# Exchanging normalised rows between partitions inside SBUF in place of through a DRAM scratch, in a fused cross-attention and LoRA-expert kernel

## The reference

```python
x = x + xattn(layernorm(x), ctx, mask)      # scores, masked softmax over 64 tokens, readout
x = x + ffn(layernorm(x), W, lora_A, lora_B, router_w)

def ffn(x, W, A, B, router_w):              # 8 experts of rank 16, the top 2 of them weighted
    base = x @ W.T                          # (1024 -> 1024)
    w_dense = renormalised top-2 of softmax(x @ router_w.T)
    Ax = einsum('nd,erd->ner', x, A)
    return base + einsum('ner,ne,eor->no', Ax, w_dense, B) * 2.0
```

## Time and profile before

| | us |
|---|---|
| median of 3 runs | 1101.16 (1099.96 to 1102.52) |
| the profiled execution | 1104.84 |
| its span | 1103.1 |
| PE matmul busy in it | 1077.6 (98%) |
| DVE busy | 750.8 (68%) |
| ACT busy | 464.5 (42%) |
| POOL busy | 114.3 (10%) |

### The profile page before, as it was taken

How to read it: one execution, slowest core, us unless ns; L and a number is a source line. 1 busy time by engine, 2 the same in 40 slices (tenths; PEclk the granted TensorE clock), 3 DMA queues, 4 the chain that set the end, 5 groups by cost and what they waited for, 6 DMA issues and landing times.

```text
span 1103.1 us, 18440 instructions
## 1 busy us (share of the span) xinstructions
PE 1077.6 (98%) x6240; PEld 1041.5 (94%) x6240; DVE 750.8 (68%) x2047; ACT 464.5 (42%) x954; POOL 114.3 (10%) x282
## 2 busy tenths in 40 slices
PE   7899999999999999999999999999999999999998
PEld 6799999999999999999999999899999999999997
DVE  6866866667666677667667677567677667666662
ACT  6544344343444453444443443443443443434330
POOL 3511001010010010010010010010010010100100
PEclk9999999999999999999999999999999999999999
DMA  9364454653545553653545534554534744435322
GB/s 325 125 220 154 153 162 146 180 189 132 177 146 159 181 183 124 194 164 131 185 159 174 190 130 136 190 190 144 189 112 156 219 147 158 135 132 191 125 87 96
DMA packets 80046, 178.92 MB, mean 162 GB/s; under 512 B 9856, under 2 KB 45184, under 8 KB 80000
## 3 DMA queue, kind: packets, MB, share of 16 engines
q1 hardware_dynamic: 79568, 176.82, 47.9%
q10 hardware_dynamic: 432, 1.57, 0.4%
HBM read 111.77 MB, written 66.58 MB: 162 GB/s over the span
## 4 chain that ended last, share of the span: by engine, by line
DVE 35%; DMA 32%; ACT 13%; SPq 6%; issue 5%; POOL 5%; PE 2%; POOLq 0%; ACTq 0%; DVEq 0%
DMA xq<-xn_dram 18%; DMA xn_dram<-xn 13%; DVE x L689 7%; DVE x2T L707 7%; DVE stats L695 7%; DVE xT_lo L714 7%; SPq L316 6%; ACT xn L484 6%; POOL rstd L393 3%; ACT xT_hi L490 3%; DVE mean_var L698 1%; ACT xT_hi L460 1%; POOL shift L396 1%; DVE var_eps L700 1%; DVE ctx_lo L603 1%
## 5 line engine op out<-in xcount | busy, mean ns | idle before, releaser
L845 PE MATMUL base_ps<-w_hi,xT_hi 128*128 128x388 f32 x1512 | 530.6, 351 | 6.9 <-DVE xT_lo L714 5.0
L846 PE MATMUL base_ps<-w_lo,xT_hi 128*128 128x388 f32 x1512 | 512.0, 339 | 0.0
L847 PE MATMUL base_ps<-w_hi,xT_lo 128*128 128x388 f32 x1512 | 511.7, 338 | 0.0
L845 PEld LDWEIGHTS base_ps<-w_hi,xT_hi 128*128 128x128 f32 x1512 | 286.2, 189 | 20.8 <-DVE xT_lo L714 5.0
L846 PEld LDWEIGHTS base_ps<-w_lo,xT_hi 128*128 128x128 f32 x1512 | 285.1, 189 | 2.7
L847 PEld LDWEIGHTS base_ps<-w_hi,xT_lo 128*128 128x128 f32 x1512 | 284.2, 188 | 0.0
L484 ACT ACTIVATE xn<-x,shift,rstd 128x1024 f32<-128x1024 f32 x63 | 78.4, 1244 | 314.8 <-POOL shift L396 314.8
L490 ACT CAST xT_hi<-x2T 128x512 fp32r<-128x512 f32 x126 | 72.0, 618 | 156.0 <-DVE x2T L707 156.0
L707 DVE STREAM_TRANSPOSE x2T<-xq 128x512 f32<-128x512 f32 x126 | 82.2, 690 | 53.6 <-DMA xq<-xn_dram 53.6
L393 POOL TENSOR_TENSOR rstd<-var_eps,neg_half 128x1 f32<-128x1 f32 x64 | 36.0, 563 | 699.8 <-DVE var_eps L700 699.8
L714 DVE TENSOR_TENSOR xT_lo<-x2T,xT_hi 128x512 fp32r<-128x512 f32 x126 | 81.4, 687 | 35.2 <-ACT xT_hi L490 34.4
(11 more groups left out here) (98 smaller groups left out, 1112.9 us busy)
## 6 DMA issues: line engine op xcount, KB each, us to landing
out<-x SPq DMA_DIRECT2D x64, 512.0 KB, 3.4
x<-in_x SPq DMA_DIRECT2D x63, 512.0 KB, 5.2
xn_dram<-xn SPq DMA_DIRECT2D x63, 512.0 KB, 2.6
xq<-xn_dram SPq DMA_DIRECT2D x252, 128.0 KB, 3.0
xT_raw<-in_xT SPq DMA_DIRECT2D x62, 512.0 KB, 4.8
ctx_raw<-in_ctx SPq DMA_DIRECT2D x16, 256.0 KB, 7.8
w_raw<-in_wT SPq DMA_DIRECT2D x8, 386.0 KB, 8.4
ctxT_raw<-in_ctxT SPq DMA_DIRECT2D x8, 256.0 KB, 7.1
```

Source lines behind the costliest of these rows:

```text
L845: pe.matmul(out_, a_hi, w_h, start=start, stop=False, skip_group_check=again)
L846: pe.matmul(out_, a_hi, w_l, start=False, stop=False, skip_group_check=again)
L847: return pe.matmul(out_, a_lo, w_h, start=False, stop=stop, skip_group_check=again)
```

## The change

The scratch is gone, and with it one of the two hops. SP waits for `xn` and at once issues four transfers from `xn` to `xq`. Each reads 1 KB from each of the 128 partitions and writes 4 KB to each of 32 partitions.

The rows are spread differently. The 128 source partitions are laid out in order over 32 partitions with four places each, so partition n of a group holds rows 4n to 4n+3. A 32x32 block, which stands for one place g, has to come out at columns g, g+4, g+8 and so on of `x2T`. The transposes of DVE therefore write with a step of four fp32 elements (16 bytes), where they wrote neighbouring elements before.

In SP's order the four transfers now stand where the transfer to the scratch stood, ahead of the store of tile t, and nothing of the exchange stands behind the store.

```diff
-            def xn_out(tile):
+            def exchange(tile):
                 sp.wait_ge(xn_done, count(tile, 1, 1))
-                sp.dma_start(xn_dram, xn[:, :]).then_inc(xn_stored, 16)
-
-            def xq_in(tile):
-                sp.wait_ge(xn_stored, count(tile, 16))
                 for a in range(Q):
                     sp.dma_start(xq[a * QP:(a + 1) * QP, :, :],
-                                 xn_dram[:, a * DQ:(a + 1) * DQ].rearrange("(g n) e -> n g e", n=QP))\
-                      .then_inc(xq_loaded, 16)
+                                 xn[:, a * DQ:(a + 1) * DQ]).then_inc(xq_loaded, 16)
...
-            xn_out((0, 1))
-            xq_in((0, 1))
+            exchange((0, 1))
...
             def step(tile):
                 b, j = tile
                 if exists(after(tile, 2)):
-                    xn_out(after(tile, 2))
+                    exchange(after(tile, 2))
                 sp.wait_ge(out_done, count(tile, G, FREE + G))
                 sp.dma_start(out[b * TPB + j], x[:, slot(tile), :]).then_inc(stored[slot(tile)], 16)
-                if exists(after(tile, 2)):
-                    xq_in(after(tile, 2))
...
             def x2_transposes(tile, i):
                 dve.wait_ge(xq_loaded, count(tile, 16 * Q))
-                out_ = x2T[:, :, :].rearrange("p c (g n) -> p g c n", n=QP)
+                out_ = x2T[:, :, :].rearrange("p c (n g) -> p g c n", g=Q)
                 dve.transpose(out_[:, i * QS:(i + 1) * QS],
                               xq[:, i * QS:(i + 1) * QS, :].rearrange("p g (c n) -> p g c n", n=QP)).then_inc(x2T_done, 1)
```

More of the change, by code:

```diff
@@ L33, in xattn_lora_moe_kernel @@
     bT_in: bass.AP,
-    xn_dram: bass.AP,
     out: bass.AP,
@@ L261, in xattn_lora_moe_kernel @@
         xn_done = sem("xn_done")
-        xn_stored = sem("xn_stored")
         xq_loaded = sem("xq_loaded")
@@ L1063 @@
     out = nc.dram_tensor("out", (B * S // P, P, O), mb.dt.float32, kind="ExternalOutput").ap()
-    xn_dram = nc.dram_tensor("xn_dram", (P, D), mb.dt.float32, kind="Internal").ap()
-    xattn_lora_moe_kernel(nc, *args, xn_dram, out)
+    xattn_lora_moe_kernel(nc, *args, out)
     r = run_bass_kernel_spmd(nc, [{f"in_{n}": a for n, a in arrays.items()}], core_ids=[0])
```

## The result

| | us |
|---|---|
| before, median of 4 runs | 1101.3 (1099.96 to 1102.52) |
| after, median of 4 runs | 1095.24 (1094.29 to 1095.95) |
| ratio | 0.9945, 95% interval 0.9928 to 0.9962 |
| forecast | 1082.6, range 1079 to 1104 |

The kernel is faster by 0.55%, a third of the 18.6 us that were forecast. The time lies in the range, near the first rival's 1092.6, and not in the forecast's own range.

What follows compares the result with a forecast made beforehand. The prediction took PE and the loop through the transfers to be in near balance. With 7.75 × (133.5 − 131.1) = 18.6 us won, 1104.84 became 1086.2, less 3.7 to the median 1082.6 us; range 1079 to 1104.

Steps and rivals of the forecast that it cites:

- first rival: VectorE's transposes: the 16-byte write step costs 0.72 us per tile, part of the gain goes, 1092.6 us; chance 0.16.
- forecast's own range: Whole kernel: 1079 to 1087 us, the range if the step costs nothing; chance 0.58.
- a loop through the transfers: Once per tile through `xn`, both hops, transposes and statistics: 16.8 us before the change, against PE's mean of about 16.4.
- PE's floor: TensorE's shortest time for eight tiles, summed from the shortest of each kind: 131.1 us, against 133.5 before the change.
- The hops: Exchange from `xn` to `xq`: dropping the scratch hop saves 2.96 us per turn, the remaining landing takes 3.0 us.
- The second loop: From `xn` over softmax, `hT_low` and transposes to the next `xn`: 126.5 us per eight tiles plus any step cost.
- δ: Extra time of a tile's two transposes from the 16-byte write step: 0, 0.72 or 1.06 us.
- the crossing at 0.88: Extra transpose time per tile, in us, at which the whole gain is eaten: 0.44 us per transpose.
- I take 0: VectorE's transposes: the forecast assumed that the 16-byte write step adds nothing to their 689 ns each.
- the nearest row of the kind: L617, a sum over 512 elements read 256 bytes apart: 1048 ns, 359 more than a transpose.
- the 0.7 at the head: Tile (0,1), where VectorE is already late: the transposes' extra time counted there once, 0.7 us.
- the sum's ends: First tile and the tile before the last: both counted as average tiles, good to about 1 us.

Runs made afterwards that it cites:

- e1: Changed kernel with the transposes writing neighbouring elements again, rows in a wrong order: 1087.13 us.
- e3: Changed kernel with the transposes writing at a step of two elements (8 bytes) in place of four, rows in a wrong order: 1086.99 us.
- e5: Changed kernel, its 16-byte step kept, with `xT_low` moved on VectorE to where it waits for the exponentials: 1085.9 us.
- e8: Changed kernel with both neighbouring writes and `xT_low` moved into the wait for the exponentials, rows in a wrong order: 1085.92 us.
- e10: Changed kernel with eight transfers per tile in place of four and transposes writing at a step of two elements, rows right: 1085.87 us.
- e2: Kernel before the change with only the transposes' writes set to a step of four elements, rows in a wrong order: 1147.94 us.
- e9: Changed kernel with the transposes writing neighbours but reading `xq` at a step of eight elements (32 bytes), rows wrong: 1109.57 us in one run.
- e6: Kernel before the change with `xT_low` moved on VectorE in front of `softmax_split`: 1097.98 us.
- e7: Changed kernel with the store of tile t put ahead of the four transfers in SP's order: 1096.34 us.

## Why the prediction was wrong, step by step

*The balance of PE and a loop through the transfers, and the gain to be had down to PE's floor.* Right. The floor of 131.1 us for eight tiles is 131.0 in e1, e3, e5, e8 and e10, and none is below it.

*The hops.* Right. With one hop VectorE doesn't wait at all; the landing's 3.5 us lies within the bounds taken. e2 shows the loop itself: 0.74 us more per tile made 45 us (1150 us expected in all, 1147.94 measured).

*The second loop, 126.5 + 8δ against 131.1.* Right in form and size. δ = 0.71 gives 132.2 (measured 132.4), δ = 0.95 gives 134.1 (measured 134.2), δ = 0 leaves PE's floor. The kernel with 0.95 is slower than the kernel before in its one run, which fits the crossing at 0.88.

*"I take 0."* This is the step that failed. It is the size of one term, 8δ: δ measured 0.71, all but the first rival's 0.72. Each transpose costs 393 ns more, beside the 359 that the nearest row of the kind gave. I set that row aside because a reduction might pay for its groups; e9 shows that a step alone costs as much or more. Between the sum's two ends the row that had a step at all was the nearer one. In eight tiles this takes 1.35 of the 2.4 us that could be won; between the changed kernel and e1 it is 9.1 us over the 62 tiles, and 8.1 in the medians. It shows where that rival looked for it, behind j = 6. With 0.71 the prediction's sum gives 7.75 × (133.5 − 132.2) = 10.1 us won, and 1091.8 us with the 0.7 at the head. So of the 12.6 us by which the forecast was missed the step explains 8 to 9, and the rest lies in the sum's ends.

*The rule of the Trainium skill.* The page "SBUF — State Buffer", section "Door 1: The DMA port swizzle", asks for two accesses to each 16-byte line. The measurements agree with that: a step of 8 bytes is free, one of 16 costs. Its wording that 4 fp32 can be strided for free doesn't hold for this instruction (1082 ns in place of 686). Nor is the price a doubling: 393 ns is 0.74 of the 532 that 512 more elements cost.

*The sum's ends.* Even with δ = 0 the forecast of 1082.6 would have been missed: e1 takes 1087.1. Of the 4.7 us between its span, 1085.5, and the forecast's (1103.1 − 18.6 − 3.7 = 1080.8), 2.8 are the start, which only the one trace showed so early. Another 3.7 are my step from the profiled execution to the median. The kernel before spreads over 1098 to 1113 us, and its profiled execution was a slower one. The spread goes with VectorE's waits for the transfers: the kernels that have them spread by 7 to 12 us in every group of six or more runs (e2 8.3, e6 12.1), and those without by 2.0 at most. So it belongs to what the change removes, and was to be taken off the gain and not off the time. No run shows why the waits vary. The kernels with PE as the bound spread over 1085.3 to 1087.5 in all groups of runs. The tiles themselves won 1.7 us more than I took, 20.3 in place of 18.6; most of it is the tile before the last, 14.22 us in place of 15.75, which I had counted as an average one.

*SP's queue and the start.* The store goes out later and nothing waits for it (e7). At the start PE waits 0.81 us for the subtraction, as before.

## What to carry to other kernels

Where PE is busy for 98% and the chain of waits still runs through transfers, measure the distances between the starts of its matmuls: the floor of each kind of tile says what can be won, and only that. Before taking a loop away, write out the next longest one with the change's own additions in it; here it was 4.6 us from binding, and a price of 0.71 us in eight places used that up. Where the only row with a cost like the change's is one that may have another reason, take the cost into the forecast or measure it alone first. In a transpose like this one keep two fp32 elements to 16 bytes, or move the cost to where the engine waits anyway: e5 won the same 9 us by moving one instruction.

## What the runs showed of the hardware

For a transpose of 128x512 fp32, a write step of 4 or 8 bytes takes 686 to 688 ns, one of 16 bytes 1082, and a read step of 32 bytes 1164. Two back to back take 1.30 us with neighbouring writes and 2.01 with the step of 16 bytes. A transfer from SBUF to SBUF of 128 KB from 128 partitions to 32 landed in 3.5 us in the median and took 602 ns to issue, where one from the DRAM scratch took 3.0 and 432. One of 64 KB from 64 partitions took 2.1 and 597. The kernel before varied by 1.4% (1098 to 1113 us) over all groups of runs, and each kernel whose VectorE doesn't wait for a transfer by 0.2% or less.
